# A graph network on one core: the record scatters cover 128 partitions instead of 125

## The chip, the cores and the metric

The kernel runs on one core of a Trainium2 chip. The metric is the device time of one launch in microseconds. The core's engines are TensorE (PE), VectorE (DVE), ScalarE (ACT), GpSimd (POOL) and SyncE (SP). SP, ACT and POOL issue DMAs; only POOL issues the indirect ones, whose row addresses come from a table in SBUF.

## The reference, cut to what matters

Two layers work on 3125 nodes of 256 values and 50000 edges `src -> dst` (sorted by `dst`), each with five attributes and a weight:

1. `x += mlp(norm(x) + sum over the edges into a node of weight * norm(x)[src])`
2. `x += mixture of 8 experts(norm(x))`, each node sent to one expert
3. `x += typed graph attention(norm(x))`: keys, queries and values by node type (19 types), a softmax over the edges by `dst` and a second one over the edges by `src`, both summed
4. `x += slice attention(norm(x))`

Steps 1 and 3 need the edges grouped by node, once in `dst` order and once in `src` order. For each edge and order the kernel makes a **record** of 128 floats (512 bytes): three time embeddings of 32 (`cos(log(t+1) w + b)`), the other node's number, its place in the window, and the weight. Only the address to which each record is written depends on the order.

## The kernel before, in words

**Where a record goes.** The edges lie in SBUF as 125 partitions (`EP`) by 400 columns (`EC`). `rank_steps` (line 313) works out on DVE and PE, for each edge, its slot in the sorted table: nodes form 25 windows of 128, each window starts on a new block of 128 rows, and there are at most 416 blocks (`NB`). The slots are copied to `slot_e[0]` (order `dst`) and `slot_e[1]` (order `src`), partitions 0 to 124 (line 369). Partitions 125 to 127 of `slot_e` keep `1 << 20`, set by two memsets of DVE (lines 2491, 2492), and no scatter reads them. The tables `rec_dst` and `rec_src` lie in DRAM (line 72).

**First stage, `embed` and `scatter_pool` (line 484).** There are 40 chunks of 10 columns. For a chunk DVE and ACT compute the embeddings and write the records of both orders into `RD[s][0]` and `RD[s][1]`, one of three buffers. DVE must wait at line 425 until the scatters of chunk c-3 have landed (`rd_sent`) before line 427 writes. ACT's sines (line 465) release POOL, which issues ten indirect DMAs (line 493), one for each column: 125 partitions, one record each, to the rows named by the column of `slot_e[0]`. SP saves the records of the other order to `rec_raw` (all 128 partitions, line 482) and writes zeros over `rec_src` piece by piece (line 476). The rank of order `src`, layer norm 1 and the type tables are worked off by DVE between the chunks. When all 400 scatters have landed, SP reads the metadata (line 540), and POOL starts the gathers of step 1 (`l0_pool`, line 579, 416 indirect DMAs of 128 partitions).

**The scatters of order `src`** (`scatter_src`, line 520, 125 partitions too) are spread over the queue of POOL: chunks 0 to 7 (80 scatters) after the gathers of step 1, beside the MLP; then `route_pool` (line 869: 25 scatters of 128 tokens to `moe_in`, waits for `slot_m`); then chunks 8 to 25 (180 scatters) beside the experts; then `expert_rows_pool` (line 994, gathers of the experts' outputs, waits for `ex_out`); then `types_pool` (line 1145), which has 10 scatters after its first group of nodes and 4 after its second; then 26 in `kvq_pool` (line 1242), one for each tile, before the tile's own scatters to `kv_tab` and `qs_tab` (lines 1257, 1259); and the last 100 in `sum_pool` (line 1613), one after each group's multiplication (line 1618), in the pass of order `dst` alone. Source buffers are loaded back from `rec_raw` with all 128 partitions. The record scatters carry no `bounds_check` argument; those of `moe_in`, `typ_x`, `kv_tab`, `qs_tab` and `y_tab` do.

**Order.** Each engine works off its queue in the order of the calls at the end of the file; counters (semaphores) tie the queues together. `consts_pool` (line 234) runs first on POOL and raises `consts` three times; DVE starts the rank after the first, PE after the second.

Of the kernel before, what the change touches and what calls it, by code (L numbers as in the profile page):

```python
# [12 lines left out]
U32 = mybir.dt.uint32  # L13
ds = bass.ds

P = 128
# [4 lines left out]
EP, EC = 125, 400  # L21
W = 25
NB = 416
U = 4
SL = 4
NG = NB // U
REC = 128
R_EQ, R_META = 64, 96
CC = 10
# [21 lines left out]
def build(nc, A, out):  # L51
    ctx = ExitStack()
    with ctx:
# [3 lines left out]
        def sem(name):  # L57
            if name not in sems:
                sems[name] = ctx.enter_context(nc.semaphore(name))
            return sems[name]  # L60

        def sb(name, shape, dt=F32):
            return ctx.enter_context(nc.sbuf_tensor(name, shape, dt))

        def dram(name, rows, cols):
            return nc.dram_tensor(name, (rows, cols), F32).ap()
# [2 lines left out]
        xn_tab = dram("xn_tab", NT * P, D)  # L69
        kv_tab = dram("kv_tab", N, KV)  # L70
        rec_raw = dram("rec_raw", NCK * P, CC * REC)
        rec_tab = [dram("rec_dst", (NB + W) * P, REC), dram("rec_src", NB * P, REC)]
        v_tab = [dram("v_dst", P, NB * PROJ), dram("v_src", P, NB * PROJ)]
        moe_in = dram("moe_in", EX * CAPP, D)
        moe_out = dram("moe_out", EX * CAPP, D)
# [24 lines left out]
        slot_e = [sb("slot_e0", [P, EC], I32), sb("slot_e1", [P, EC], I32)]  # L100
# [11 lines left out]
        def ar(off, *shape, dt=F32):  # L112
            n = 1
            for k in shape:
                n *= k
            v = AR[:, off:off + (n // 2 if dt is BF16 else n)]
            if dt is not F32:
                v = v.bitcast(dt)
            if len(shape) == 2:
                v = v.rearrange("p (a b) -> p a b", b=shape[1])  # L120
            if len(shape) == 3:
                v = v.rearrange("p (a b c) -> p a b c", b=shape[1], c=shape[2])
            return v
# [35 lines left out]
        RB = (4, 2)  # L159
        RD = [[ar(7200 + 2560 * s + 1280 * o, CC, REC) for o in range(2)] for s in range(3)]  # L160
        R2 = [ar(9600 + 1280 * j, CC * REC) for j in range(4)]
        CL, CK = 27, 30
        EARLY = 4
        R2T = [BIGR[:, NT * SROW + CC * REC * j:NT * SROW + CC * REC * (j + 1)] for j in range(4)]

# [68 lines left out]
        def consts_pool(pool):  # L234
            pool.memset(ident[:, :], 0.0)
            pool.memset(tri[:, :], 1.0)
            pool.memset(ones[:, :], 1.0)
            pool.iota(iota1[:, :], [[1, P]], base=1, channel_multiplier=0, allow_small_or_imprecise_dtypes=True)
            pool.iota(iotaz[:, :], [[1, P]], base=0, channel_multiplier=0, allow_small_or_imprecise_dtypes=True)
            pool.iota(pcol[:, :], [[0, 1]], base=0, channel_multiplier=1, allow_small_or_imprecise_dtypes=True)  # L240
            pool.iota(jrow, [[1, NB]], base=0, channel_multiplier=0, allow_small_or_imprecise_dtypes=True)
            pool.drain()
            pool.affine_select(out=ident[:, :], in_=ident[:, :], compare_op=ALU.not_equal, fill=1.0, base=0,
                               pattern=[[-1, P]], channel_multiplier=1)
            pool.affine_select(out=tri[:, :], in_=tri[:, :], compare_op=ALU.is_gt, fill=0.0, base=0,
                               pattern=[[1, P]], channel_multiplier=-1)
            pool.drain()
            pool.tensor_copy(identb[:, :], ident[:, :])
            pool.tensor_copy(trib, tri[:, :])
            for k in range(2):  # L250
                pool.tensor_copy(TRI2[:, 32 * k:32 * k + 32], tri[:, 0:32])
            pool.drain()
            pool.tensor_copy(rk[:, 4, 2:3], iotaz[:, 0:1]).then_inc(sem("consts"), 1)
            pool.memset(BASE2, 0.0)
            pool.memset(PICK, 0.0)
            pool.memset(SPRD, 0.0)
            pool.drain()
            for k in range(2):
                pool.affine_select(out=PICK, in_=PICK, compare_op=ALU.not_equal, fill=1.0, base=-32 * k,
                                   pattern=[[-1, W], [1, 64]], channel_multiplier=0)  # L260
                pool.affine_select(out=SPRD, in_=SPRD, compare_op=ALU.not_equal, fill=1.0, base=-32 * k,
                                   pattern=[[-1, W], [0, P]], channel_multiplier=1)
                pool.drain()
            pool.tensor_copy(rk[:, 4, 0:1], iotaz[:, 0:1]).then_inc(sem("consts"), 1)
            for s in range(3):
                for o in range(2):
                    pool.memset(RD[s][o], 0.0)
            pool.drain()
            pool.tensor_copy(rk[:, 4, 1:2], iotaz[:, 0:1]).then_inc(sem("consts"), 1)
# [20 lines left out]
        def clear_scalar(act):  # L290
            act.wait_ge(sem("zeros"), 1)
            v = rec_tab[0].rearrange("(b p) c -> p b c", p=P)[:, FULL:NB, :]
            act.dma_start(v, ZR[:, 0:REC].unsqueeze(1).to_broadcast([P, NB - FULL, REC])).then_inc(sem("zeroed"), 16)

# [189 lines left out]
        def scatter_pool(pool):  # L484
            pool.wait_ge(sem("slots"), 1)
            pool.wait_ge(sem("zeroed"), CLEARED)
            for c in range(NCK):
                s = c % 3
                pool.wait_ge(sem("sin_done"), c + 1)
                pool.wait_ge(sem("rd_meta"), 2 * c + 2)  # L490
                pool.nop(nofuse=True)
                for k in range(CC):
                    pool.indirect_dma_start(  # L493
                        rec_tab[0], bass.IndirectOffsetOnAxis(ap=slot_e[0][0:EP, c * CC + k:c * CC + k + 1].bitcast(U32), axis=0),
                        RD[s][0][0:EP, k, :], None,
                    ).then_inc(sem(f"rd_sent{s}"), 16)

        def scatter_src_pool(pool, c0, c1):

            if c0 == 0:  # L500
                pool.wait_ge(sem("slots"), 2)
                pool.wait_ge(sem("zeroed_src"), 16 * NCK)
                pool.wait_ge(sem("l0_mm"), NG)
                for s in range(3):
# [14 lines left out]

        def scatter_src(pool, c, k, buf):  # L520
            pool.indirect_dma_start(  # L521
                rec_tab[1], bass.IndirectOffsetOnAxis(ap=slot_e[1][0:EP, c * CC + k:c * CC + k + 1].bitcast(U32), axis=0),
                buf[0:EP, k * REC:(k + 1) * REC], None,
            ).then_inc(sem(f"r2_sent{c % 4}"), 16)

        META_EDGE = (0, 2) + tuple(range(8, NG + 1, 8))
        MP0 = len(META_EDGE) - 1
# [28 lines left out]
        def pipe(stages):  # L556
            lead = max(ahead for ahead, _ in stages)
            for k in range(-lead, NG):
                for ahead, f in stages:
                    if 0 <= k + ahead < NG:  # L560
                        f(k + ahead)
# [7 lines left out]
        def l0_pool(pool):  # L569
            pool.wait_ge(sem("xn_tab"), 16)  # L570
            for g in range(NG):
                s = g % SL
# [10 lines left out]
        def l0_vector(ve):  # L583
# [27 lines left out]
            weights(1)  # L611
            for g in range(NG):
                if g + 2 < NG:
# [1499 lines left out]
        def slice_clear_vector(ve):  # L2113
            ve.memset(BDS, 0.0)
            ve.memset(BDM, 0.0)
            ve.drain()
            ve.memset(BDM[0:G, 0:G], 1.0)
            ve.memset(BDM[G:P, G:P], 1.0)
            ve.drain()
            ve.tensor_scalar(BDM, BDM, BIG, -BIG, ALU.mult, ALU.add).then_inc(sem("ffn_clear"), 1)  # L2120
# [365 lines left out]
        @block.vector  # L2486
        def _(ve):
            ve.memset(ZR, 0.0).then_inc(sem("zeros"), 1)
            ve.memset(NTY[:, 24:26], 0)
            ve.memset(X[:, 24:NT, :], 0.0).then_inc(sem("zeros"), 1)  # L2490
            ve.memset(slot_e[0][:, :], 1 << 20)
            ve.memset(slot_e[1][:, :], 1 << 20)
            ve.wait_ge(sem("ids"), 32)
            ve.wait_ge(sem("consts"), 1)
            for _ in rank_steps(ve, 0):
                pass
            embed_vector(ve, rank_steps(ve, 1))
            l0_vector(ve)
            ve.drain()
            mlp_vector(ve)  # L2500
            route_vector(ve)
            experts_vector(ve)
            expert_rows_vector(ve)
            kvq_vector(ve)
            for o in range(2):
                score_vector(ve, o)
                if o:
                    slice_clear_vector(ve)
                sum_vector(ve, o)
            proj_vector(ve)  # L2510
            norm_vector(ve)
            slices_vector(ve)
            tokens_vector(ve)
            final_vector(ve)
# [33 lines left out]
```

## Time and profile before

| | us |
|---|---|
| median of 3 runs (lowest, highest) | 4536.61 (4534.31, 4543.26) |
| the profiled execution | 4545.78 |
| its span, first to last instruction | 4544.0 |
| mean granted TensorE clock | 0.759 of full speed |
| busy: PE, DVE, ACT, POOL | 2851.6, 2430.3, 1721.8, 2903.1 |

The page gives the time of each engine, the chain of waits and the groups of instructions. In the groups a line such as L493 is the line of the kernel, `xcount` the number of instructions, then busy time and the mean of one in ns. "Issue" before an instruction is time in which its engine waited for nothing that the profile shows.

### The profile page before, as it was taken

To read this page: it belongs to the slowest core of one execution; us is meant where nothing else is said; L and a number is where in the kernel's file an instruction comes from. 1 tells how busy PE (TensorE), PEld (TensorE's weight loads), DVE (VectorE), ACT (ScalarE), POOL (GpSimd) and SP (SyncE) were. 2 spreads that over 40 slices of the span, in tenths; PEclk is the share of its full clock that TensorE was granted. 3 is DMA by queue.
4 is the path that set the end of the run, shared out by engine and by line. 5 is a ranking of instruction groups with operands and counts; after the bars stand their busy time and mean duration, and the time that the engine had idled before them with its cause. 6 is when DMAs were issued, how large, how long until landed. Compare 5 with 4: busy or idle time off the path is not lost.

```text
span 4544.0 us, 51396 instructions
## 1 busy us (share of the span) xinstructions
PE 2851.6 (63%) x13692; PEld 1930.3 (42%) x13692; DVE 2430.3 (53%) x4965; ACT 1721.8 (38%) x4345; POOL 2903.1 (64%) x2661
## 2 busy tenths in 40 slices
PE   3200004545563990676777778996777777996598
PEld 1000003433352660234444446884444445885455
DVE  7534444445452114336777775556777776666353
ACT  1222310000021121124555556774555555885451
POOL 5777786666667887665555556996555553555641
PEclk6555556677776995687777778997777778997898
DMA  4444448433345662677667675877876665665300
GB/s 136 135 130 136 131 133 208 124 89 93 93 88 165 209 193 80 212 212 229 202 207 210 203 199 149 207 194 190 213 206 206 209 204 143 172 173 135 101 1 29
DMA packets 805878, 720.82 MB, mean 159 GB/s; under 512 B 424289, under 2 KB 700363, under 8 KB 805468
## 3 DMA queue, kind: packets, MB, share of 16 engines
q1 hardware_dynamic: 645116, 399.08, 30.9%
q0 software_dynamic: 153536, 315.11, 24.6%
q10 hardware_dynamic: 6944, 3.34, 0.3%
q8 instruction: 119, 1.95, 0.2%
q14 instruction: 163, 1.34, 0.1%
HBM read 482.09 MB, written 241.99 MB: 159 GB/s over the span
## 4 chain that ended last, share of the span: by engine, by line
DVE 21%; POOL 16%; another core or an unknown queue 12%; PE 11%; issue 10%; ACT 7%; DVEq 4%; DMA 1%; ACTq 1%; SPq 1%; POOLq 0%
POOL rec_src L521 9%; DVE META L1380 8%; POOL AR L1618 4%; DVE AR L1400 4%; DVE BIGR L605 3%; ACT AR L1674 2%; DVEq L1396 2%; DVE AR L596 2%; DVE AR L1393 2%; ACT AR L1676 1%; PE ps L1217 1%; PE ps L2390 1%; ACTq L1675 1%; PE ps L1428 1%
## 5 line engine op out<-in xcount | busy, mean ns | idle before, releaser
L1349 POOL DMA_INDIRECT AR<-kv_tab,META x832 | 793.7, 954 | 594.8 <-DVE AR L1393 330.1
L493 POOL DMA_INDIRECT rec_dst<-AR,slot_e x400 | 489.1, 1223 | 169.2 <-issue 169.2
L1380 DVE TENSOR_REDUCE META<-ps 128x8 f32<-128x1024 f32 x416 | 508.1, 1222 | 83.7 <-remote 58.6
L625 PE MATMUL ps<-AR 128*128 128x256 f32 x832 | 313.1, 542 | 354.8 <-DVE AR L596 147.4
L579 POOL DMA_INDIRECT AR<-xn_tab,META x416 | 398.0, 957 | 199.8 <-issue 130.2
L1618 POOL TENSOR_TENSOR AR<-AR 128x896 f32<-128x896 f32 x208 | 352.4, 1694 | 235.2 <-ACT AR L1683 232.4
L1583 DVE TENSOR_TENSOR BIGR<-BIGR,ps 128x260 f32 x832 | 354.3, 426 | 229.1 <-PE ps L1657 144.3
L1657 PE MATMUL ps<-AR 128*128 128x260 f32 x1664 | 420.1, 396 | 12.0 <-POOL AR L1618 5.6
L521 POOL DMA_INDIRECT rec_src<-AR,slot_e x290 | 353.3, 1218 | 91.6 <-issue 88.0
L1478 PE MATMUL ps<-AR,identb 128*128 128x512 bf16 x832 | 404.5, 486 | 7.7 <-issue 5.2
L625 PEld LDWEIGHTS ps<-AR 128*128 128x128 f32 x832 | 216.3, 273 | 452.4 <-issue 236.0
L1480 PE MATMUL ps<-AR 128*128 128x512 bf16 x832 | 400.8, 482 | 0.0
L1393 DVE TENSOR_TENSOR AR<-AR,ps 128x896 f32<-128x896 f32 x208 | 225.4, 1084 | 278.0 <-remote 259.1
L1526 ACT ACTIVATE AR<-ps 12x512 bf16<-12x512 bf16 x208 | 122.1, 587 | 648.3 <-remote 455.0
L605 DVE TENSOR_TENSOR BIGR<-BIGR,ps 128x256 f32 x416 | 175.1, 421 | 306.7 <-remote 175.4
L1657 PEld LDWEIGHTS ps<-AR 128*128 128x128 f32 x1664 | 302.9, 192 | 64.9 <-POOL AR L1618 26.2
L1457 PEld LDWEIGHTS ps<-QS,AR 128*128 128x128 f32 x1664 | 268.1, 244 | 22.4 <-issue 17.1
L1457 PE MATMUL ps<-QS,AR 128*128 x1664 | 275.9, 323 | 0.0
L1674 ACT ACTIVATE AR<-iota,META 128x128 f32<-128x128 f32 x832 | 263.5, 391 | 28.4 <-DVE AR L1420 28.4
L1504 ACT ACTIVATE AR<-iota,META 128x128 f32<-128x128 f32 x832 | 262.4, 385 | 24.1 <-DMA META<-rec_src 16.8
L749 ACT ACTIVATE AR<-ps 128x256 f32<-128x256 f32 x25 | 9.5, 381 | 681.6 <-PE ps L706 675.1
L774 PE MATMUL ps<-BIGR,tri 128*128 128x494 f32 x2 | 2.0, 1110 | 414.7 <-DVE BIGR L1099 414.7
(430 smaller groups left out, 5851.2 us busy)
## 6 DMA issues: line engine op xcount, KB each, us to landing
v_dst<-AR SPq DMA_DIRECT2D x104, 384.0 KB
AR<-v_dst SPq DMA_DIRECT2D x104, 384.0 KB
v_src<-AR SPq DMA_DIRECT2D x104, 384.0 KB
AR<-v_src SPq DMA_DIRECT2D x104, 384.0 KB
AR<-in_W_qvk SPq DMA_DIRECT2D x44, 608.0 KB
rec_raw<-AR SPq DMA_DIRECT2D x40, 640.0 KB, 3.3
AR<-rec_dst SPq DMA_DIRECT2D x104, 192.0 KB
AR<-rec_src SPq DMA_DIRECT2D x104, 192.0 KB
```

The source lines that it names most:

```text
L493: pool.indirect_dma_start(rec_tab[0], bass.IndirectOffsetOnAxis(ap=slot_e[0][0:EP, c * CC + k:c * CC + k + 1].bitcast(U32), axis=0), RD[s] ...
L521: pool.indirect_dma_start(rec_tab[1], bass.IndirectOffsetOnAxis(ap=slot_e[1][0:EP, c * CC + k:c * CC + k + 1].bitcast(U32), axis=0), buf[0 ...
L579: pool.indirect_dma_start(GA[s][:, u, :], None, xn_tab, bass.IndirectOffsetOnAxis(ap=META[0][:, g * U + u, 0:1].bitcast(U32), axis=0)).the ...
L625: ins = pe.matmul(l0_ps(s, u), OW[s][:, u, :], GA[s][:, u, :], start=True, stop=True)
L1349: pool.indirect_dma_start(KVR[s][:, u, 0:KV], None, kv_tab, bass.IndirectOffsetOnAxis(ap=META[o][:, g * U + u, 0:1].bitcast(U32), axis=0)) ...
L1380: ve.tensor_reduce(BMALL[o][:, g * U + 2 * half:g * U + 2 * half + 2, :].rearrange("p b h -> p (b h)"), PSA[:, 2048 + 1024 * half:3072 + 1 ...
L1457: pe.matmul(q[:, u, 0:DK], OTF[g % 2][:, u, :], QS[:, ds(ws[u], 1), :].rearrange("p t d -> p (t d)"), start=False, stop=False, skip_group_ ...
L1478: pe.matmul(PS[4 + u], identb[:, :], NEG[g % SL][:, u, :].unsqueeze(1).to_broadcast([P, H1, P]), start=True, stop=False, skip_group_check= ...
L1480: ins = pe.matmul(PS[4 + u], SEL[:, u, :], ATB[g % 2], start=False, stop=True, skip_group_check=True)
L1618: pool.tensor_tensor(v, v, VB[s][:, :, D:SROW].unsqueeze(3).to_broadcast([P, U, H1, DK]), ALU.mult).then_inc(sem("pv"), 1)
L1657: pe.matmul(PS[4 + u][:, 0:SROW], OH[s][:, u, :], VB[s][:, u, :], start=True, stop=True).then_inc(sem("sum"), 1)
L1674: act.activation(DIST2[g % 2][:, u, :], iota1[:, :], ACT.Abs, scale=-1.0, bias=META[o][:, g * U + u, 1:2])
```

## The change

Both record scatters take all 128 partitions of their source and of `slot_e`. The three idle partitions need an address: `slot_e` is filled by two iotas of POOL with `NB*P - 125 + partition + 3*column`, so that partitions 125 to 127 of the 400 columns name 1200 different rows from row `NB*P` on, behind the blocks that are read. `rec_dst` has 25 blocks there already; `rec_src` gets 16 more. What is written there (the zeros of `RD`'s idle partitions, or what `rec_raw` kept of them) is read by nobody. The two memsets of DVE go. Neither version passes a bounds check to these scatters.

```diff
+SPARE = 16
-        rec_tab = [dram("rec_dst", (NB + W) * P, REC), dram("rec_src", NB * P, REC)]
+        rec_tab = [dram("rec_dst", (NB + W) * P, REC), dram("rec_src", (NB + SPARE) * P, REC)]
...
             pool.iota(jrow, [[1, NB]], base=0, channel_multiplier=0, allow_small_or_imprecise_dtypes=True)
+            for o in range(2):
+                pool.iota(slot_e[o][:, :], [[P - EP, EC]], base=NB * P - EP, channel_multiplier=1)
             pool.drain()
...
-                        rec_tab[0], bass.IndirectOffsetOnAxis(ap=slot_e[0][0:EP, c * CC + k:c * CC + k + 1].bitcast(U32), axis=0),
-                        RD[s][0][0:EP, k, :], None,
+                        rec_tab[0], bass.IndirectOffsetOnAxis(ap=slot_e[0][:, c * CC + k:c * CC + k + 1].bitcast(U32), axis=0),
+                        RD[s][0][:, k, :], None,
...
-                rec_tab[1], bass.IndirectOffsetOnAxis(ap=slot_e[1][0:EP, c * CC + k:c * CC + k + 1].bitcast(U32), axis=0),
-                buf[0:EP, k * REC:(k + 1) * REC], None,
+                rec_tab[1], bass.IndirectOffsetOnAxis(ap=slot_e[1][:, c * CC + k:c * CC + k + 1].bitcast(U32), axis=0),
+                buf[:, k * REC:(k + 1) * REC], None,
...
-            ve.memset(slot_e[0][:, :], 1 << 20)
-            ve.memset(slot_e[1][:, :], 1 << 20)
```

The zeroing of `rec_src` in `raw_sync` follows the size of the table: 54 pieces of 1024 floats for each partition instead of 52, still in 40 DMAs.

## Rows read from the trace of the kernel before

**Rows 1.** Page: busy us of each engine; chain of waits, 1290 to 1745 us
```profile
PE 2851.6 (63%) x13692; PEld 1930.3 (42%) x13692; DVE 2430.3 (53%) x4965; ACT 1721.8 (38%) x4345; POOL 2903.1 (64%) x2661
...
by line: POOL rec_src L521 68.5%; issue 22.6%; POOL moe_in L872 5.4%; POOL AR L514 3.1%; DMA AR<-rec_raw 0.9%; POOL BIGR L998 0.2%; POOLq L872 0.2%; POOLq L516 0.1%; POOLq L505 0.0%; POOLq L870 0.0%
```

**Rows 2.** Both record scatters' lines: ns min/median/max, idle before (us, times), who waited
```profile
L493 POOL DMA_INDIRECT rec_dst<-AR,slot_e x400: 1186/1190/7149, 77.1 to 686.6; - x134
...
  issue: 169.2, 400
...
  DVE AR L427: 261.8, 37
...
L521 POOL DMA_INDIRECT rec_src<-AR,slot_e x290: 1186/1190/2752, 1302.3 to 1919.6; - x145
```

**Rows 3.** The same view for other indirect transfers, all of 128 partitions
```profile
L872 POOLq MOVE  x25: 29/29/38, 1409.9 to 1442.4; - x25
L872 POOL DMA_INDIRECT moe_in<-XNW,slot_m x25: 980/980/1027, 1427.2 to 1458.1; - x25
...
L1259 POOL DMA_INDIRECT qs_tab<-AR,TID x44: 977/983/1025, 1852.3 to 2025.9; - x44
...
L579 POOL DMA_INDIRECT AR<-xn_tab,META x416: 951/957/1014, 692.7 to 1284.6; - x139
```

**Rows 4.** Timeline, first stage, POOL and DVE (start us, us, what, idle before)
```profile
78.83 1.19 POOL L493 DMA_INDIRECT rec_dst<-AR,slot_e  x1 [0.30 <-issue]
...
98.33 1.16 DVE L427 SCALAR_TENSOR_TENSOR AR<-AR,ps 125x960 f32<-125x960 f32 x1 [4.30 <-DMA rec_dst<-AR,slot_e]
...
643.79 1.15 DVE L427 SCALAR_TENSOR_TENSOR AR<-AR,ps 125x960 f32<-125x960 f32 x1 [2.23 <-DMA rec_dst<-AR,slot_e]
...
686.55 1.19 POOL L493 DMA_INDIRECT rec_dst<-AR,slot_e  x1 [0.30 <-issue]
692.68 1.00 POOL L579 DMA_INDIRECT AR<-xn_tab,META  x1 [4.93 <-issue]
```

**Rows 5.** Timeline of the start of the kernel
```profile
1.82 0.47 POOL L241 IOTA BIGR<- 128x416 f32 x1
...
3.03 0.39 DVE L2492 MEMSET slot_e<- 128x400 int32 x1
...
6.55 2.44 DVE L315 TENSOR_SCALAR BIGR<-AR 125x400 int32<-125x400 int32 x1 [3.13 <-DMA AR<-in_src]
```

**Rows 6.** Timeline from routing to the experts' outputs
```profile
1407.22 0.18 DVE L865 CAST slot_m<-AR 128x26 int32<-128x26 f32 x1
...
1427.17 1.03 POOL L872 DMA_INDIRECT moe_in<-XNW,slot_m  x1 [0.30 <-issue]
...
1720.06 0.38 DVE L1136 TENSOR_SCALAR BIGR<-iotaz 128x26 f32<-128x26 f32 x1 [5.35 <-DMA moe_out<-AR]
...
1743.78 0.99 POOL L998 DMA_INDIRECT BIGR<-moe_out,rowof_m  x1 [0.30 <-issue]
```

**Rows 7.** Timeline at the type scatters; waits of 1845 to 2028 us
```profile
1795.54 3.55 ACT L1006 ACTIVATE BIGR<-X,nmr,rs 128x256 f32<-128x256 f32 x7 [10.38 <-DVE nmr L1035]
...
1803.51 1.08 POOL L1150 DMA_INDIRECT typ_x<-BIGR,slot_t  x1 [0.30 <-issue]
...
ACT AR L1240 <- remote: 22.3, 6, 5.2
POOL kv_tab L1257 <- ACT AR L1240: 19.7, 9, 3.3
```

**Rows 8.** POOL in the two sum passes: period with scatters, then without
```profile
3079.85 1.23 POOL L521 DMA_INDIRECT rec_src<-BIGR,slot_e  x1 [0.19 <-issue]
...
3082.99 1.23 POOL L521 DMA_INDIRECT rec_src<-BIGR,slot_e  x1 [0.19 <-issue]
...
3839.95 1.69 POOL L1618 TENSOR_TENSOR AR<-AR 128x896 f32<-128x896 f32 x1 [1.37 <-ACT AR L1683]
3843.00 1.69 POOL L1618 TENSOR_TENSOR AR<-AR 128x896 f32<-128x896 f32 x1 [1.37 <-ACT AR L1683]
```

## The prediction

> **What bounds the kernel.** I began with the page: no engine is busy much over three fifths of the span, and POOL (2903.1 us) stands beside PE (2851.6) [rows 1]. So the stages had to be read one by one, and the question for each was whether POOL's queue of scatters is what the next step waits for. The chain of waits for 1290 to 1745 us answers it for the middle: 68.5% of that stretch is line 521, and most of the 22.6% "issue" is the pause before each such DMA [rows 1]. The chain cannot be followed through the first stage, so there I read the timeline. POOL issues one record scatter after another, 1.19 us each with 0.30 us before it [rows 4], and the pauses of all 400 come to 169.2 us, of which 47.6 are the wait before the first [rows 2]. DVE is idle before line 427 in 37 of 40 chunks, 261.8 us in all, always until scatters land [rows 2]: it has 4.3 us to spare in an early chunk, 7.1 on the mean, and 2.2 in the last [rows 4]. The stage is POOL's queue, 1.49 us at a time, from 77 to 688 us.
>
> **What a scatter costs.** The reader should set two views side by side. The record scatters take 1190 ns at the median, in either table [rows 2]. The other indirect transfers, of 128 partitions, take 980 ns (scatter to moe_in, 1024 bytes a row), 983 (scatter to qs_tab, 224 bytes a row) and 957 (gather of 1024 bytes) [rows 3]. So neither direction nor length of the row makes 1190; a row of 512 bytes lies between those lengths. What is left is the count of partitions, 125 against 128. A bounds check cannot be the reason: the scatters to moe_in carry one (it shows as a 29 ns MOVE beside each), the gathers carry none, and both are cheap [rows 3]. No row shows a scatter of 128 rows without a check. It is bounded by 951 ns (the shortest gather) and 983 ns (scatter with a check); an outer bound is today's 1190. I take 957, that of the gather, since it too carries no check. Each scatter then saves 1.190 - 0.957 = **0.233 us** of POOL's queue; with 983 it would be 0.207. The pause of 0.30 us is the same for all and stays.
>
> The Trainium skill ("DMA: Bandwidth & Descriptors", section on why a DMA increments its semaphore by 16) says that a DMA is dealt to the largest number of DMA engines up to 16 that divides its slowest dimension: 5 engines for 125 rows, 16 for 128. It gives no price on POOL's queue for that, and no row here splits a scatter by engine, so it enters no term; it only says why 125 could be an awkward number.
>
> **The terms, in order of time.**
>
> 1. *Start.* Two iotas are added on POOL, at 0.47 us for 416 columns [rows 5] some 0.9 us together, ahead of the releases of DVE and PE. Two memsets of 0.39 us leave DVE, which then idles 3.13 us until the edge ids land before its first rank step at 6.55 [rows 5]. The rank on DVE covers both. First scatter at 77 us as before: 0. The lower bound is no gain, the upper cost 0.9 us.
> 2. *First stage*, 400 scatters: 400 x 0.233 = 93.2. POOL's chunk goes from 14.9 to 12.6 us, 2.3 less, below DVE's 4.3 to spare. The last chunk has only 2.2 us, but POOL is then three chunks behind DVE: line 427 of the last chunk is at 643.8, the last scatter at 686.6 [rows 4]. Its data are there in time. The meta read and the 4.9 us before the first gather stay. Two more zero pieces of 512 KB go on SP's queue, whose DMAs nobody waits for here: 0.
> 3. *Chunks 0 to 7*, 80 scatters: 80 x 0.233 = 18.6. `slot_m` is there at 1407.4, POOL takes the first routed scatter at 1427.17 [rows 6]: 19.8 us late, so all 18.6 counts, with 1 us left before DVE's routing becomes the wait.
> 4. *Chunks 8 to 25*, 180 scatters: POOL would save 41.9. But the experts' outputs have landed at 1720.06 (DVE starts on them), and POOL reads them from 1743.78 [rows 6]. It is 23.7 us late, and more cannot be won: 23.4, and POOL waits for the experts thereafter. The experts start when moe_in is full, so they carry term 3 along.
> 5. *Types*, 14 scatters: 14 x 0.233 = 3.3. ACT has the second group ready at 1799.1, POOL takes it at 1803.5 [rows 7].
> 6. *K, V and Q*, 26 scatters, at most 26 x 0.233 = 6.1. A tile with a scatter costs POOL 1.19 + 0.98 + 0.98 + 0.9 = 4.1 us. POOL waits for ACT 19.7 us in 9 places, ACT for others' transfers 22.3 in 6 [rows 7]: both bound it by turns. I take half, 3.0.
> 7. *Sum over dst*, 100 scatters: the period is 3.14 us, POOL without a gap beyond the pauses; in the sum over src, without scatters, the same work has a period of 3.05, and POOL idles 1.37 in each [rows 8]. With 0.23 less POOL falls to 2.9, under 3.05. So only 0.09 x 100 = 9 is won, and some 2 for the seven reloads between: 11, not 23.
>
> Sum: 93.2 + 18.6 + 23.4 + 3.3 + 3.0 + 11 = **152.5 us**. Against the profiled execution (4545.8 us, 4544.0 of it span) that is 4393.3; it lies 9.2 over the median of the runs, and against the median I say 4536.6 - 152.5 = **4384**. At 983 ns terms 2, 3 and 5 shrink to 82.8, 16.6 and 2.9, the sum is about 139, and the time 4398. With 951 ns, all of term 6 and 13 in term 7 it is about 161, 4376. Stages between (gathers of step 1, both score passes) issue no record scatter and should keep their lengths.
>
> **Rivals.** *Priced by the row (slower).* If POOL pays for each row it describes, and the difference to the others has another cause, 128 rows cost 1.190 x 128/125 = 1.219 us, 0.029 more. On the path lie the 400, 80, 180, 14, 26 and 100 scatters: 800 x 0.029 = 23 us, 4560. It decides from the first point at which 128 rows do cost more than 125, with POOL's queue as the place. Against it: 128 rows are cheaper everywhere else [rows 3]. Chance 0.05.
>
> *The price stays (no change).* The records' own tables or index columns make the 1190 ns, and the count of rows is neither good nor bad: 4537, the change doing nothing that it could. The Trainium skill (same page, section "Anatomy of one DMA") says that many descriptors can be emitted before their number shows; by that rule alone 3 rows more or less change nothing, and the time would be this one. For it speaks that all record scatters share their index layout; against it, that every other table, index and row length gives 951 to 983. Chance 0.05.
>
> *The middle does not follow.* Scatters at a quicker pace crowd the experts' weights, and the outputs land later in proportion. No row of the sum speaks for it, but none shows that pace either. Then terms 4 and 6 are lost, 26 us: 4411, or 4430 if term 3 goes as well. Chance 0.12.
>
> **How the numbers follow.** The forecast takes 0.78. Its own range runs from 4376 to 4398, and 9 us on either side for the spread of the three runs. To 4425 it takes in most of the third case. Two in ten left outside are the two cases near 4537 and 4560, tails of the third and gains beyond the terms: range **4364 to 4425**. About 0.2% (9 us) is what a measurement of this kernel can tell from no change. Faster by more: 0.90, the forecast and the third case; same 0.05; slower 0.05.
>
> **What would show it.** In the changed profile: both record scatters at about 957 ns (983 at most) with 0.30 between; the last line-493 scatter near 594 us instead of 687; DVE's idle before line 427 down from 262 to about 180 us; the first routed scatter within 1 us or so of `slot_m`; POOL waiting some 18 us for moe_out before its first gather of it; line 1618 waiting for ACT in the sum over dst, period 3.05. The forecast is wrong if the scatters still take 1.19 us or more, if DVE becomes the wait of the first stage, or if the saved time comes back as a longer experts' stage.

## The result, and the profile after

The changed kernel takes **4742.0 us** (median of 4 runs, 4738.2 to 4749.3) beside 4539.1 for the kernel before (4534.3 to 4543.3, 4 runs): a ratio of 1.0453, 95% interval 1.0438 to 1.0469. The forecast was 4384 with a range up to 4425, and it gave "slower" a chance of 0.05. The profiled execution has a span of 4737.7 us, 193.7 more than that of before.

The page of the changed kernel has the busy time of each engine and the DMA queues; the line by itself is the queue of POOL on the page of before:

```profile
PE 2871.0 (61%) x13692; PEld 1934.0 (41%) x13692; DVE 2420.5 (51%) x4963; ACT 1719.8 (36%) x4345; POOL 2702.3 (57%) x2663
...
q0 software_dynamic: 115136, 315.46, 23.0%
```

```profile
q0 software_dynamic: 153536, 315.11, 24.6%
```

POOL is 200.8 us less busy than before [rows 1], and its queue sends 38400 packets fewer than before, 48 for each of 800 record scatters. So the change did to the scatters what it should, and the kernel is 203 us longer. The lines of POOL's DMAs (ns min/median/max, first and last start in us) show both halves of that:

```profile
L496 POOL DMA_INDIRECT rec_dst<-AR,slot_e x400: 952/958/5104, 77.7 to 661.4; - x134
L582 POOL DMA_INDIRECT AR<-xn_tab,META x416: 940/946/1035, 666.6 to 1261.2; - x139
L524 POOL DMA_INDIRECT rec_src<-AR,slot_e x290: 952/958/1732, 1274.3 to 2130.2; - x145
L524 POOL DMA_INDIRECT rec_src<-BIGR,slot_e x110: 959/1002/1045, 2137.5 to 3282.5; - x110
L875 POOL DMA_INDIRECT moe_in<-XNW,slot_m x25: 983/985/1000, 1469.2 to 1500.2; - x25
L1001 POOL DMA_INDIRECT BIGR<-moe_out,rowof_m x25: 942/948/1732, 1959.9 to 1993.3; - x25
L1352 POOL DMA_INDIRECT AR<-kv_tab,META x832: 940/946/1477, 2239.7 to 3985.2; - x167
```

A record scatter costs 958 ns in place of 1190 [rows 2], as forecast. The first and last starts cut the span into stages (lines are 3 higher than before; the row of before's line 1349 follows):

```profile
L1349 POOL DMA_INDIRECT AR<-kv_tab,META x832: 943/951/1536, 2028.9 to 3787.8; - x167
```

| stretch | before | after | difference | forecast |
|---|---|---|---|---|
| to the last dst scatter | 686.6 | 661.4 | -25.2 | -93 |
| to the first src scatter | 615.7 | 612.9 | -2.8 | 0 |
| chunks 0 to 7, to the first moe_in scatter | 124.9 | 194.9 | **+70.0** | -18.6 |
| moe_in, chunks 8 to 25, to the first gather of moe_out | 316.6 | 490.7 | **+174.1** | -23.4 |
| types, K, V, Q, to the first kv gather | 285.1 | 279.8 | -5.3 | -6.3 |
| score pass and sum over dst, to the last src scatter | 1054.1 | 1042.8 | -11.3 | -11 |
| to the end | 1461.0 | 1455.2 | -5.8 | 0 |

The loss sits in two stages, those in which POOL issues src scatters back to back while PE, ACT and DVE do other work. POOL's waits from 1270 to 1970 us in the changed kernel (us in total, times, longest):

```profile
POOL BIGR L1001 <- DMA moe_out<-AR: 212.3, 1, 212.3
POOL moe_in L875 <- DVE slot_m L868: 89.7, 1, 89.7
```

POOL is done early and then waits: 89.7 us for the routing, 212.3 for the experts. So the others are late. The busy time of the engines from 1510 to 1740 us, after and then before (us, PE, PEld, DVE, ACT, POOL, clock, DMA share, GB/s), has the experts' stage in both:

```profile
1510.00:1740.00 230.00, 66.57 (x120) 31.17 (x119) 2.23 (x4) 6.69 (x10) 171.60 (x186) 0.55 0.36 122
```

```profile
1510.00:1740.00 230.00, 191.19 (x697) 128.48 (x695) 25.33 (x43) 38.65 (x57) 185.79 (x160) 0.95 0.59 179
```

PE does 120 matmuls where it did 697, and the DMA engines move less than before. Of PE's waits in this stage none is for the experts' weights. PE's timeline in the middle of that stretch:

```profile
1642.05 0.58 PE L947 MATMUL ps<-BIGR 128*128 128x256 f32 x1 [2.22 <-issue]
1644.85 0.58 PE L947 MATMUL ps<-BIGR 128*128 128x256 f32 x1 [2.22 <-issue]
1647.65 0.58 PE L947 MATMUL ps<-BIGR 128*128 128x256 f32 x1 [2.22 <-issue]
```

One matmul each 2.80 us, and "issue" before it: nothing that the profile knows of holds PE. A weight load lies between two of them, so PE gets one instruction per 1.4 us. POOL itself is held at the end of this burst of scatters:

```profile
1743.07 0.96 POOL L524 DMA_INDIRECT rec_src<-AR,slot_e  x1 [0.44 <-issue]
1745.17 0.96 POOL L524 DMA_INDIRECT rec_src<-AR,slot_e  x1 [1.14 <-issue]
1746.57 0.96 POOL L524 DMA_INDIRECT rec_src<-AR,slot_e  x1 [0.44 <-issue]
```

Its scatters come 1.40 or 2.10 us apart there, where most came 1.26 apart before 1680 us. From 1640 to 1720 us PE's matmuls start 2.10, 2.80 or 3.50 us apart and nothing between, so all these steps are multiples of 0.70 us. From 1755.6 on PE, ACT and DVE run at full pace again. I call this *starving* below. The granted clock averages 0.55 from 1510 to 1740 us (0.95 in the kernel before), but it follows PE's idling and does not lead it: from 1595 to 1600 us it is still 0.82 while PE does a single matmul, and then it falls to 0.50, the lower level.

### The profile page after: what moved, and what is told of

Read it like the earlier page. It is cut to its first block, busy times and chain, and to the rows that moved or that the text cites. A ratio compares the mean times of both kernels' runs of the same rounds, so it can differ in the third digit from the quotient of the medians.

```text
span 4737.7 us, 51396 instructions
## 1 busy us (share of the span) xinstructions
PE 2871.0 (61%) x13692; PEld 1934.0 (41%) x13692; DVE 2420.5 (51%) x4963; ACT 1719.8 (36%) x4345; POOL 2702.3 (57%) x2663
## 3 DMA queue, kind: packets, MB, share of 16 engines
q0 software_dynamic: 115136, 315.46, 23.0%
## 4 chain that ended last, share of the span: by engine, by line
PE 21%; another core or an unknown queue 19%; DVE 16%; ACT 11%; issue 10%; DVEq 3%; ACTq 2%; POOL 2%; DMA 1%; SPq 1%; POOLq 0%
DVE META L1383 5%; ACT AR L1677 3%; DVE BIGR L608 3%; PE ps L1660 2%; DVE AR L1403 2%; PE ps L947 2%; PE ps L936 2%; ACT AR L1679 2%; ACT AR L1507 2%; DVE AR L599 2%; ACTq L1678 1%; PE ps L1431 1%; DVEq L1399 1%; PE ps L628 1%
## 5 line engine op out<-in xcount | busy, mean ns | idle before, releaser
L496 POOL DMA_INDIRECT rec_dst<-AR,slot_e x400 | 395.4, 988 | 236.6 <-issue 170.5
L524 POOL DMA_INDIRECT rec_src<-AR,slot_e x290 | 281.1, 969 | 99.6 <-issue 95.9
L1403 DVE TENSOR_REDUCE AR<-AR 128x16 f32<-128x896 f32 x208 | 225.8, 1086 | 34.0 <-issue 33.7
```

Of the source, the lines that this page charges most:

```text
L496: pool.indirect_dma_start(rec_tab[0], bass.IndirectOffsetOnAxis(ap=slot_e[0][:, c * CC + k:c * CC + k + 1].bitcast(U32), axis=0), RD[s][0] ...
```

## The experiments

All "PE" figures below are the idle time "issue" before the experts' 512 matmuls of the second layer (line 947 in the changed kernel): the shortest sign of starving, though not its whole price. x3, x7, x8 and x11 leave records out of the table; they are there for their traces alone.

**1. What about the scatter starves the others?** Four kernels on one chip (kernel before there: 4533.4).

```
x1: 128 rows, slot_e filled with 1 << 20 again (no iota),
+   bounds_check=..., oob_is_err=False      on both scatters
x2: src: slot_e[1][0:EP, ...], buf[0:EP, ...]    (125 rows; dst 128)
x3: src: slot_e[1][0:120, ...], buf[0:120, ...]  (dst 128)
x4: after every record scatter:
+   pool.drain()
+   pool.iota(padz[:, :], [[1, 96]], ...)
```

> Idle rows of all 800 record scatters hold an index outside the table and a bounds check drops them; nothing goes to spare rows. Three theories. SPARE: the writes to the spare rows (or the missing check) stall PE, ACT and DVE during POOL's bursts; then the stalls go, line 524 costs about 983 ns, and the time falls to about 4398. WIDTH: what stalls the others is that a scatter of 128 rows is dealt over all 16 DMA engines; then PE in the experts' stage still does one matmul per 2.8 us and the time stays within 4700 to 4790. PACE: it is the shorter period of the scatters (1.26 us in place of 1.49); with 1.29 us the stalls stay too, perhaps a little milder, 4680 to 4790.

4738.3 us, ratio 1.0451 (1.0421 to 1.0482), with 977 ns for a scatter. Same time, same stalls (PE's "issue" 101.0 us): neither the spare rows nor the missing check has a part in it.

> Only the 400 scatters to rec_dst cover 128 rows; the 400 to rec_src go back to 125 with the same index tile. All theories: the experts' stage and the MLP stage are as in the kernel before (PE 0.22 us per matmul, slot_m about 138 us after the first src scatter). What is left is the first stage, 25 us shorter in the changed kernel: about 4510 (4500 to 4520). If it is over 4536, the 128-row scatters of the first stage or the iotas do damage that outlasts them.

4511.2 us, 0.9951 (0.9932 to 0.9971). So all of the loss comes from the src scatters; the dst scatters alone gain, but 22 us and not 93.

> The src scatters cover 120 rows (rows 120 to 124 of each column are left out of the table); dst keeps 128. WIDTH, in the form that the number of DMA engines decides: if 120 rows use 15 of them, the stalls stay nearly whole, 4700 to 4790. In the form that it takes all 16 of them: the stalls go, about 4400. PACE: as the time of one scatter stays 0.95 to 1.0 us, the stalls stay, 4700 to 4790. SPARE: rows 125 to 127 are no longer written, the stalls go, about 4400.

4743.9 us, 1.0464. A scatter costs 987 ns, and PE's "issue" is 83.1 us. The spare rows are out again, and all 128 rows are not needed either.

> After each of the 800 record scatters POOL drains and writes a small iota, some 0.3 us, so that the period is 1.5 us or more, that of the kernel before or longer, at 128 rows. PACE: the stalls go, PE runs at 0.22 us per matmul in the experts' stage, and the time is about that of the kernel before, 4540 to 4600 by how long the filler is. WIDTH and SPARE: the stalls stay and POOL's own queue is longer on top: 4750 to 4900.

6044.9 us. The filler was far longer than meant; the timeline of the first stage shows why:

```profile
299.33 0.98 POOL L498 DMA_INDIRECT rec_dst<-AR,slot_e  x1 [0.46 <-issue]
301.76 0.20 POOL L503 IOTA padz<- 128x96 f32 x1 [1.46 <-issue]
302.43 0.98 POOL L498 DMA_INDIRECT rec_dst<-AR,slot_e  x1 [0.46 <-issue]
```

The drain behind a scatter takes 1.46 us, and the period is 3.1. But PE's stalls are gone (rows of the experts' matmuls, busy us and mean ns, idle before; the kernel after first, then x4):

```profile
L947 PE MATMUL ps<-BIGR 128*128 128x256 f32 x512 | 129.1, 402 | 101.5 <-issue 100.7 <-ACT BIGR L965 0.8
```

```profile
L953 PE MATMUL ps<-BIGR 128*128 128x256 f32 x512 | 112.6, 381 | 0.8 <-ACT BIGR L971 0.8
```

With 128 rows and spare rows as in the changed kernel, at a slow pace, nobody starves. That speaks for pace, too coarsely to prove it.

**2. Pace, width or bytes.** A second chip (kernel before: 4535.6). Dst has 128 rows in all four.

```
x5: after each src scatter
+   pool.iota(slot_e[0][0:32, CC*c+k:CC*c+k+1], [[1, 1]], ...)
x6: after each src scatter
+   for q in range(4): pool.nop(nofuse=True)
x7: src: slot_e[1][0:124, ...]
x8: src: slot_e[1][0:64, ...]
```

> After each of the 400 src scatters (128 rows, as in the changed kernel) POOL writes a column of one element per partition into the dst index tile, which nobody reads any more. By the 0.47 us of 416 columns and the 0.20 us of 96 it should take 0.12 to 0.15 us, so the period goes from 1.26 to about 1.4 us. PACE (the stalls come from the shorter period): between 1.26 (stalls) and 1.49 (none) there is a point at which they end; if 1.4 is beyond it, PE in the experts' stage is back at 0.22 us per matmul and the time near 4510. WIDTH (16 or 15 DMA engines for one scatter, whatever the period): the stalls stay, 4700 to 4800.

4695.8 us, 1.0352 (1.0271 to 1.0433). The timeline shows a scatter each 1.31 to 1.32 us, and here PE gets its matmuls some 1.4 us apart:

```profile
1601.71 0.98 POOL L524 DMA_INDIRECT rec_src<-AR,slot_e  x1 [0.17 <-issue]
1602.26 0.50 PEld L949 LDWEIGHTS ps<-BIGR 128*128 128x128 f32 x2 [1.81 <-issue]
1602.27 1.21 PE L949 MATMUL ps<-BIGR 128*128 128x256 f32 x2 [0.83 <-issue]
1602.71 0.15 POOL L529 IOTA slot_e<- 32x1 int32 x1
...
1603.02 0.98 POOL L524 DMA_INDIRECT rec_src<-AR,slot_e  x1 [0.17 <-issue]
```

PE's "issue" is 33.8 us in place of 100.7: 0.06 us more per scatter takes two thirds of it away. The time tells another story: of the 207 us lost only 47 come back. The experts' stage still takes 459.0 us (489.8 in x6), because ACT comes late instead: PE waits 81 us for it, 52 in x6. Most of the 0.15 us of padding is hidden: the pause before the next scatter shrinks from 0.30 to 0.17.

> Four empty instructions after each src scatter in place of the column: a second way to lengthen the period, without any memory access. No row has their price; if each takes 0.03 to 0.06 us the period is 1.4 to 1.5 us. PACE: stalls shrink or go as in the padded kernel, in step with the period that the trace shows. WIDTH: 4700 to 4800.

4742.9 us, 1.0456. The four empty instructions lie within the pause of 0.30 us; the period stays at 1.26 us, and so does the time. A null test by accident: these extra instructions on POOL change nothing, as the pace doesn't change.

> Src scatters cover 124 rows (row 124 of each column is left out), dst 128. If POOL's price goes by how many DMA engines share the rows, as 120 rows (995 ns) and 128 rows (958 ns) against 125 (1190 ns) suggest, 124 rows on 4 engines cost 1.19 us or more, and with that period PACE and WIDTH both say no stalls: about 4511, that of the kernel with 125. If it costs about 0.96 us, the price went by something else and PACE says stalls, 4700 or more.

4550.0 us, 1.0027 (1.0011 to 1.0043); no stalls (PE's "issue" 0), and each scatter costs 1308 ns: one row fewer than 125, and dearer by 118 ns.

> Src scatters cover 64 rows: half the rows and bytes (61 rows of each column are left out of the table), still dealt over 16 DMA engines, 4 rows each. WIDTH by engines alone, or PACE: stalls as before, over 4650, more if a scatter gets cheaper than 0.95 us. If it is the bytes or rows per unit of time that crowd something out, halving them ends the stalls: 4400 to 4500.

4746.1 us, 1.0463. Half the rows and half the bytes starve PE all the same ("issue" 83.8 us), at 897 ns a scatter and 1.20 us between starts. It isn't the bytes. The number of packets did not fall with them (115136 on POOL's queue, as with 128 rows), so this run says nothing on packets.

**3. A longer padding, and a chip that does not starve.** The fillers rotate through four places of the dst index tile, which is free by then. Each raises a semaphore, and POOL waits for that of two fillers before.

```
x9:  +  pool.iota(slot_e[0][:, 100 * i:100 * i + 100], ...)   after each src scatter
x10: +  two such, of 60 columns
x11: src: slot_e[1][0:5, ...]
```

> After each src scatter of 128 rows POOL writes 100 columns of the dst index tile (nobody reads it any more), some 0.2 us, so the period should be 1.37 to 1.45 us (1.31 in the kernel with one column, which cut the loss only from 203 to about 160 us). PACE: the stalls shrink much further or end, 4510 to 4600. WIDTH: the kernel with one column was a coincidence of 40 us and the stalls stay: 4690 or more.

> Two such writes of 60 columns after each src scatter: the period should be 1.5 to 1.65 us, longer than in the kernel before (1.49), still 128 rows over 16 DMA engines. PACE: no stalls; PE 0.22 us per matmul in the experts' stage; the time 4511 or a little above, by what POOL's longer period costs (at 0.1 us more than 1.49, up to 40 us). WIDTH: stalls, 4700 or more.

> The src scatters cover 5 rows: 5 DMA engines, one row each (120 rows of each column are left out of the table). The price should fall below 0.9 us, the period below 1.2. PACE alone: the stalls come although the width is that of the kernel before, 4650 or more. WIDTH (more than 5 engines are needed): no stalls, and with POOL quicker than in any other kernel the time is 4400 to 4480.

This third chip is different: the kernel **before** takes 4122.3 us on it (4116.0 to 4124.0, 3 runs), 413 less than on the others. x9 takes 3981.2 (0.9661, 0.9633 to 0.9689), x10 4013.7 (0.9740, at 1.48 us per scatter), x11 4311.4 (1.0463). By that alone they could not separate pace from width, since the chip had changed with them. x11's own time says little: its second score pass, the one that reads the nearly empty table, takes 897 us where x9's takes 527. But its PE has no "issue" in the experts' stage at a period of about 1.16 us: on this chip not even that pace starves anyone. The dst scatters of these kernels are those of the changed kernel, unpadded. Their row, and DVE's row of the wait, in x9:

```profile
L496 POOL DMA_INDIRECT rec_dst<-AR,slot_e x400: 954/958/7426, 77.7 to 597.4; - x134
```

```profile
L430 DVE SCALAR_TENSOR_TENSOR AR<-AR,ps 125x960 f32<-125x960 f32 x40 | 46.2, 1154 | 179.2 <-DMA rec_dst<-AR,slot_e 178.8
```

The forecast had "near 594 us" and "about 180 us" for these two. With 125 rows on the same chip (z1, below) the last dst scatter is at 685.8.

**4. The same padded kernel on a chip that starves.** A fourth chip (kernel before: 4570.7, 18 runs).

```
y1: the changed kernel    y2: x9's kernel    y3: the kernel before    y4: x2's kernel
```

> The changed kernel once more, beside the kernel before on whatever chip this is. The kernel before took 4534 to 4543 us on three chips and 4122 us on a fourth. STARVED: on the three chips something holds back the instruction flow of PE, DVE and ACT (pauses with no wait behind them), in the kernel before already, and quicker scatters only make that worse. Then on a chip where the kernel before takes about 4122 the changed kernel gains nearly what was forecast: 3950 to 3985; where it takes about 4535, the changed one takes 4735 to 4750. SCATTER: the loss comes from the scatters themselves on any chip; then about 4320 where the kernel before takes 4122.

4778.2 us, 1.0435 (1.0384 to 1.0485): the loss of the changed kernel again.

> The padded kernel that took 3981 us beside 4122, src period about 1.41 us. STARVED with PACE: on a 4535 us chip the longer period brings the src stages back, about 4500 to 4560; on a 4122 us chip again 3981, and the changed kernel without padding is 10 to 30 us quicker than this one. If on a 4535 us chip it takes 4700, pace is not what decides.

4564.4 us, 0.9999 (0.9978 to 1.0020). This is the run that **tells pace from width**: the 128-row scatter of the changed kernel, but one each 1.39 us (1.40 in the pair shown),

```profile
1602.22 0.97 POOL L526 DMA_INDIRECT rec_src<-AR,slot_e  x1 [0.17 <-issue]
...
1603.21 0.23 POOL L533 IOTA slot_e<- 128x100 int32 x1
...
1603.62 0.97 POOL L526 DMA_INDIRECT rec_src<-AR,slot_e  x1 [0.17 <-issue]
```

and the experts' matmuls are back at their length, with 4.1 us of "issue" in place of y1's 100.5 on the same chip:

```profile
L954 PE MATMUL ps<-BIGR 128*128 128x256 f32 x512 | 113.7, 380 | 4.1 <-issue 4.1
```

```profile
L947 PE MATMUL ps<-BIGR 128*128 128x256 f32 x512 | 128.9, 401 | 101.3 <-issue 100.5 <-ACT BIGR L965 0.8
```

0.13 us of added period per scatter gives 214 us back. That it is the period and not the presence of a POOL instruction between two scatters follows from x5, whose filler is of the same kind but shorter and helps in part only, and from x6. Nor is it the pause between scatters: that is 0.30 us in x2, which does not starve, as in the changed kernel, which does. Not all is back at 1.39 us: the stretch of chunks 0 to 7 takes 151.1 us, where it takes 124.5 in the kernel before on this chip (y3) and 117.0 in x9.

> The kernel before, unchanged, for its trace on this chip. On a 4122 us chip: line 1349 on POOL waits about 12 us for DVE line 1393 (330 us in the trace shown), DVE's 259 us of idle without a known releaser before line 1393 are gone, and the first stage with 125-row scatters keeps its length (last scatter at 687 us, 1.49 us each). On a 4535 us chip: as in the trace shown.

4570.9 us, 0.9997, in the main the expectation's second case: its first score pass takes 704.9 us (691.1 in the trace of before), but DVE's idle time without a known releaser before line 1393 is 169.3 us, not 259.1.

> dst with 128 rows, src with 125. On a 4122 us chip the first stage gains 93 us by its trace and the time is about 4030; on a 4535 us chip 4511 again, the first stage gaining only 25.

4550.8 us, 0.9955 (0.9937 to 0.9974): x2's gain again.

x9 and y2 are one program on two chips, 583 us apart. The first dst stage ends at 597.4 against 660.8. The larger part lies where nobody had changed anything, at the unpadded gathers. DVE's row of line 1403 (line 1393 of before) on the two chips, y2 and then x9:

```profile
L1403 DVE TENSOR_TENSOR AR<-AR,ps 128x896 f32<-128x896 f32 x208 | 225.1, 1082 | 184.2 <-remote 162.1 <-PE ps L1469 15.6 <-DMA AR<-kv_tab,META 6.4
```

```profile
L1403 DVE TENSOR_TENSOR AR<-AR,ps 128x896 f32<-128x896 f32 x208 | 224.6, 1080 | 22.4 <-PE ps L1469 10.4 <-DMA AR<-kv_tab,META 9.8 <-issue 2.1
```

and POOL's row of the 832 gathers, with the last gather of the first pass on each chip (y2, then x9):

```profile
L1359 POOL DMA_INDIRECT AR<-kv_tab,META x832 | 788.0, 947 | 616.8 <-DVE AR L1403 339.4 <-issue 266.7 <-DMA v_dst<-AR 5.5
...
2727.75 0.95 POOL L1359 DMA_INDIRECT AR<-kv_tab,META  x1 [0.30 <-issue]
```

```profile
L1359 POOL DMA_INDIRECT AR<-kv_tab,META x832 | 788.5, 948 | 268.7 <-issue 245.6 <-DVE AR L1403 12.2 <-PE ps L1667 3.1
...
2344.51 0.95 POOL L1359 DMA_INDIRECT AR<-kv_tab,META  x1 [0.30 <-issue]
```

Where the chip starves, DVE sits idle for an unknown releaser ("remote") and POOL in turn waits for DVE; the first score pass takes 699.6 us (from 2028.1), on the other chip 523.3 (from 1821.2).

**5. Pacing the gathers as well.** If gathers 1.25 us apart starve the others in the kernel before too, padding them should speed that kernel up on a starving chip.

```
z1: the kernel before; after each kv_tab gather  + pool.iota(slot_e[0][:, ...100 columns], ...)
z2: the changed kernel; the same after kv_tab and xn_tab gathers and all record scatters (60 columns for dst)
z3: as z2, 50 columns everywhere
```

> The kernel before with one edit of mine: after each of the 832 gathers of the two score passes (128 rows, no check, 1.26 us apart while POOL has nothing to wait for) POOL writes 100 columns of a tile that is free by then, so that they come at most every 1.41 us. PACE on a chip where the kernel before takes about 4535: the gathers starve DVE, ACT and PE in the kernel before already (a pass takes 691 us there, 524 us on the 4122 us chip); with the padding a pass is bound by 416 x 1.41 = 587 us, 100 less, twice: about 4335 to 4360. If only scatters starve the others: no gain, 4530 to 4580. On a 4122 us chip: 2 x 60 us slower, about 4240.

> The changed kernel with the padding behind every record scatter and every gather of step 1 and of the score passes (100 columns, 60 behind the dst scatters). PACE on a 4535 us chip: src stages as in the padded kernel before (4564 beside 4571), score passes 2 x 100 us shorter, first stage and step 1 some 20 us shorter together: 4330 to 4370, faster than both kernels. On a 4122 us chip: 3981 + 120 + about 100 for the first two stages: 4200.

> The same with 50 columns everywhere: about 0.05 us less per DMA, 1.36 us. If the point at which the others are starved lies below 1.36, another 50 to 90 us less than with 100 columns, 4250 to 4300 on a 4535 us chip; if it lies above, part of the stalls is back, 4380 to 4560. On a 4122 us chip some 90 us less than with 100 columns.

The three ran on the chip that does not starve (kernel before: 4113.4), so they tell only what padding costs: z1 4182.6 (1.0166, 1.0133 to 1.0200), z2 4138.5 (1.0060, 1.0037 to 1.0083), z3 4067.1 (0.9886, 0.9857 to 0.9914). z1 costs 69 us, not the 120 expected, since 100 columns bring the gathers to 1.36 us and not 1.41. z2 and z3 are 157 and 86 us over x9, which has padding behind the src scatters alone. Whether pacing the gathers pays on a starving chip was **not** measured.

## Why the prediction was wrong

**Right: the price.** "Both record scatters at about 957 ns with 0.30 between": 958 and 0.30. The runs also fit a rule that the forecast left out. By the Trainium skill ("DMA: Bandwidth & Descriptors", section on why a DMA increments its semaphore by 16) 124, 125, 120, 128, 64 and 5 rows are dealt as 31, 25, 8, 8, 4 and 1 rows to an engine. The medians, in that order, are 1308, 1190, 987, 958, 897 and 854 ns: some 14 ns per row of one engine up to 25 rows, 20 beyond, and 29 more where 15 engines share what 16 could. No trace shows the split over engines itself. By the Trainium skill (same page, section "Anatomy of one DMA") many descriptors can be emitted before their number shows; here it shows early, 854 ns for 5 rows and 897 for 64.

**Right: the start and the last terms.** The first scatter is at 77.7 (0.6 later); types with K, V and Q gained 5.3 where terms 5 and 6 had 6.3; term 7, with its cap by ACT instead of 23 us, gave 11.3 where it had 11, with line 1621 waiting for ACT at a period of 3.05 us as foreseen. Two small slips change nothing: the terms at 983 ns add up to 139.7 (4397), and term 6 took ACT's 22.3 us "remote" for waits on transfers, while the label says only that the releaser is not known.

**Wrong: terms 2, 3 and 4.** The step that failed is the overlap that all three share. Each took POOL's queue as shorter by 0.233 us per scatter and everything beside it as unchanged ("POOL's chunk goes from 14.9 to 12.6 us, 2.3 less, below DVE's 4.3 to spare"). DVE's slack was real only at the instruction rate of before. At 1.26 us per DMA the rate falls: in term 2 DVE's wait for scatters falls to 88.3 us, far below the 180 forecast, because DVE and ACT come late themselves. ACT's row has 184.7 us of "issue" before its sines, where before's wait was for DVE alone:

```profile
L468 ACT ACTIVATE AR<-AR 125x320 f32<-125x320 f32 x240 | 90.6, 455 | 400.0 <-DVE AR L430 215.3 <-issue 184.7
```

Of 93 us 68 are lost. In terms 3 and 4 the forecast had -42 and the result is +244. The forecast's last sign of being wrong came true: the saved time came back as a longer experts' stage, 490.7 us where it had 316.6. On the chip that does not starve term 2 came out within 4 us (597.4), so its arithmetic was right and its premise was not.

**The rivals.** *Priced by the row* ended on the slower side, with the wrong mechanism and the wrong sign: 128 rows cost 232 ns less than 125. *The price stays* was refuted by the same 958 ns. *The middle does not follow* had the right place, and the right condition ("none shows that pace"), at 0.12. It was sized at 26 to 45 us, still a gain, and blamed the experts' weights; the DMA share fell instead of rising. What it lacked was a price for a quicker pace.

**A sign of that price stood in the trace of before.** The gathers of the score passes were issued at that pace already, and DVE's row of line 1393 there, 

```profile
L1393 DVE TENSOR_TENSOR AR<-AR,ps 128x896 f32<-128x896 f32 x208 | 225.4, 1084 | 278.0 <-remote 259.1 <-PE ps L1459 11.2 <-DMA AR<-kv_tab,META 6.5
```

has 259.1 us of idle time with no known releaser, while nothing of the kind stands beside the scatters 1.49 us apart: there line 427 of DVE waits for the scatters themselves [rows 2]. It is a sign and not the price (y3 has 169.3 us in its place), and that the gathers cause it was not tested. The forecast compared the prices of scatters and gathers [rows 3], but not what the other engines did beside each.

**What is shown and what is open.** The runs on the chips that starve, by the commonest time from one src scatter to the next (the two stages are those of the table of stretches that grew, all in us):

| run | rows | period | chunks 0 to 7 | moe_in to moe_out | PE's "issue" |
|---|---|---|---|---|---|
| x8 | 64 | 1.20 | 194.0 | 489.8 | 83.8 |
| changed kernel | 128 | 1.26 | 194.9 | 490.7 | 100.7 |
| x1 | 128 | 1.28 | 194.1 | 490.2 | 101.0 |
| x3 | 120 | 1.29 | 193.2 | 490.2 | 83.1 |
| x5 | 128 | 1.32 | 186.1 | 459.0 | 33.8 |
| y2 | 128 | 1.39 | 151.1 | 312.6 | 4.1 |
| x2 | 125 | 1.48 | 123.9 | 315.8 | 0 |
| kernel before | 125 | 1.49 | 124.9 | 316.6 | 0 |
| x7 | 124 | 1.61 | 135.6 | 336.5 | 0 |

Shown: with 128 rows the starving goes with the time between POOL's indirect DMAs. It is more of a step than a slope: from 1.20 to 1.29 us the stages are equal within 2 us, at 1.32 a part is back, at 1.39 nearly all. (The periods beyond are those of other row counts; with 128 rows on a starving chip the next one is x4's 3.1.) It needs no spare rows, no missing check, and not all the rows and bytes. Shown too: it depends on where the program runs, since one program took 3981 us on one chip and 4564 on another, and the kernel before took 4122 and 4113 us in two sets of runs on the first. Open: what the chips differ in; what it is that instructions of PE, ACT, DVE and at last POOL wait for in steps of 0.70 us; whether the recording of the instructions takes part, since every time in this document is of an execution recorded in that way; whether scatters of 5 rows would starve anyone on a starving chip (x11 fell on the other one); and what the changed kernel itself takes on the chip that does not starve. x9 is the changed kernel plus padding and gained 141 us there, so a gain is likely but was not run.

**A version that beats both.** Dst with 128 rows and src with 125 was faster than the kernel before on two starving chips, by half a per cent (0.9951 and 0.9955, both intervals below 1). With 128 rows and 1.39 us between src scatters the time is unchanged on a starving chip (0.9999) and 3.4% shorter on the other.

## What to carry to other kernels

Before shortening POOL's DMAs, find a stage of the same trace in which POOL already issues at the new pace, and read what PE, DVE and ACT do beside it: idle time by "issue" or "remote" in the shadow of back-to-back indirect DMAs is a warning that slack there may not be real. If a stage is not bound by POOL, a slower or padded sequence can be the faster one, and 0.13 us more per scatter was worth 214 us here. A gain that rests on one chip's trace should be timed on several.

## What was not expected of the hardware

The same kernel takes 4113 to 4122 us on one chip and 4533 to 4571 on others. In one padded program on both, the 832 gathers take 948 and 947 ns and DVE's line 1403 1080 and 1082: the instructions are as long, and the idle time differs. Indirect DMAs of POOL 1.20 to 1.29 us apart hold PE to one instruction per 1.4 us on the latter, whether they carry 64 or 128 rows; at 1.39 us hardly any of that is left. PE's starts then lie 2.10, 2.80 or 3.50 us apart, all multiples of 0.70. A POOL drain behind an indirect DMA took 1.46 us. And of the numbers of rows near 128 that ran, 128 was the cheapest: a scatter took 958 ns on POOL's queue with 128 rows, 987 with 120, 1190 with 125 and 1308 with 124.
